# Causal attention: triangular masks taken from TensorE and given to GpSimd and VectorE

## The reference, cut to what matters

```python
q = (x @ Wq.T).reshape(B, S, H, hd).transpose(0, 2, 1, 3)   # k and v alike
scores = jnp.einsum('bhcd,bhsd->bhcs', qi, k) * scale
mask = kpos[None, :] <= qpos[:, None]
scores = jnp.where(mask, scores, jnp.finfo(scores.dtype).min)
p = jax.nn.softmax(scores, axis=-1)
return (None, jnp.einsum('bhcs,bhsd->bhcd', p, v))
```

## Time and profile before

| | |
|---|---|
| median of 3 executions | 2668.89 us (2668.31 to 9096.91) |
| span of the profiled execution | 2692.8 us |
| TensorE / VectorE / ScalarE / GpSimd busy | 91% / 69% / 52% / 30% |
| attention: head and groups | 151 to 224 us, 224 to 1156 us |

### The profile page before, as it was taken

One profiled execution on the slowest core, in us unless ns is written; L12 is line 12 of the kernel. 1 busy time (PEld: TensorE's weight loads), 2 busy tenths in 40 slices (PEclk: granted clock), 3 DMA queues, 4 the chain that ended last, 5 costly groups with the idle time before them and its releaser, 6 DMA issues. The chain is left out here.

```text
span 2692.8 us, 51134 instructions
## 1 busy us (share of the span) xinstructions
PE 2451.3 (91%) x16420; PEld 1589.0 (59%) x16420; DVE 1846.2 (69%) x3682; ACT 1406.8 (52%) x2776; POOL 815.1 (30%) x647
## 2 busy tenths in 40 slices
PE   5648999999999999969977599999999999999999
PEld 4512333333333333358866477777777777777777
DVE  7757877877787777424438476777667767766776
ACT  3404655656565566755634255555555555555554
POOL 1070000000000000014425355554455555444553
PEclk9858999999999999989988699999999999999999
DMA  4574041321404040033257000000000000000000
GB/s 135 191 170 65 5 62 26 41 52 16 61 6 62 6 60 5 7 127 133 102 177 241 18 13 12 11 13 13 13 13 13 9 11 13 13 13 13 13 9 9
DMA packets 189865, 132.85 MB, mean 49 GB/s; under 512 B 99857, under 2 KB 177687, under 8 KB 189712
## 3 DMA queue, kind: packets, MB, share of 16 engines
q1 hardware_dynamic: 160048, 100.06, 15.4%
q10 hardware_dynamic: 24160, 14.16, 2.2%
q0 software_dynamic: 5504, 16.69, 1.7%
HBM read 84.43 MB, written 46.14 MB: 48 GB/s over the span
## 5 line engine op out<-in xcount | busy, mean ns | idle before, releaser
L859 DVE TENSOR_REDUCE a_best<-a_ring 128x1 f32<-128x512 f32 (+3 forms) x1280 | 700.9, 604 | 214.0 <-PE a_ring L721 123.0
L836 ACT ACTIVATE a_probs<-a_pss 128x1024 f32<-128x1024 f32 (+3 forms) x640 | 554.0, 895 | 452.6 <-PE a_pss L777 228.7
L721 PE MATMUL a_ring<-a_kb,a_qa 96*128 96x512 bf16 (+3 forms) x1280 | 453.0, 365 | 67.2 <-DVE a_best L859 32.3
L774 PE MATMUL a_pss<-a_qa,a_kb 99*128 99x512 bf16 (+3 forms) x1280 | 433.9, 353 | 15.6 <-issue 7.2
L1771 ACT ACTIVATE w_probs<-w_pss,w_top 128x256 f32<-128x256 f32 x512 | 239.0, 476 | 379.7 <-DVE w_top L1859 365.0
L1606 POOL TENSOR_TENSOR w_probs<-w_probs,w_inv 128x512 f32<-128x512 f32 x256 | 301.0, 1176 | 395.7 <-DVE w_inv L1865 386.3
L962 POOL TENSOR_TENSOR e_w_r<-e_w,e_w_r 128x1024 fp32r<-128x1024 f32 x28 | 67.0, 2402 | 1032.7 <-ACT e_w_r L1035 1032.7
L1629 PE MATMUL w_psw<-wqkv,w_xr 128*128 128x512 f32 x1152 | 301.5, 398 | 11.6 <-POOL w_xr L1563 11.6
L774 PEld LDWEIGHTS a_pss<-a_qa,a_kb 99*128 99x128 bf16 x1280 | 123.5, 98 | 302.6 <-ACT a_probs L836 224.5
L792 PE MATMUL a_acc<-a_probs,a_vg 128*32 128x512 f32 (+3 forms) x2560 | 299.9, 541 | 0.1
L1669 PE MATMUL w_pss<-w_kd,w_qt 128*128 128x256 f32 x1536 | 278.4, 310 | 0.0
(11 more groups left out here) (223 smaller groups left out, 3771.2 us busy)
## 6 DMA issues: line engine op xcount, KB each, us to landing
e_w<-in_w SPq DMA_DIRECT2D x16, 1024.0 KB, 7.9
qk_parts<-p_parts SPq DMA_DIRECT2D x32, 384.0 KB, 3.7
a_qa<-qk_parts SPq DMA_DIRECT2D x192, 64.0 KB, 2.5
a_kb<-qk_parts SPq DMA_DIRECT2D x42, 256.0 KB, 9.5
p_xin<-in_x SPq DMA_DIRECT2D x8, 512.0 KB, 5.4
v_rows<-p_vout SPq DMA_DIRECT2D x8, 512.0 KB, 5.1
a_vg<-v_rows SPq DMA_DIRECT2D x32, 128.0 KB, 9.1
expert_in<-zero POOLq DMA_DIRECT2D x16, 256.0 KB, 8.3
```

Source lines behind the costliest of these rows:

```text
L721: ins = pe.matmul(bank[:, 0:keys], qa[u][0:QR, i // TC, h, (i % TC) * P:(i % TC + 1) * P], kb[u][0:QR, h, k * CH:k * CH + keys], start=Tru ...
L774: ins = pe.matmul(pss[idx % 2][:, e, lo:CH], kb[u][0:MR, h, j * P:(j + 1) * P], qa[u][0:MR, c, h, lo:CH], start=True, stop=(j < TC * c))
L836: act.activation(probs[:, idx % 4, :, lo:CH], pss[idx % 2][:, :, lo:CH], ACT.Exp).then_inc(exp_done, 1)
L859: vec.tensor_reduce(best[:, i // TC, h * TC + i % TC, k:k + 1], bank[:, 0:keys], X, ALU.max).then_inc(ring_taken, 1)
```

## The change

Masking leaves TensorE in both places.

- `mask_kq` is gone. Scores on the diagonal are exponentiated unmasked, and GpSimd then sets the entries of future keys in `probs` to zero with `affine_select`, one per pair of heads (2 x 128 columns), behind a one-element add that carries the wait for the exponential. Products on the diagonal wait for `future_cleared` instead of `exp_done`.
- The maxima's diagonal block is masked on VectorE: a reduction over the columns ahead of the block (one column where there are none), then `tensor_tensor_reduce`: PSUM block plus `mask_qk` (now fp32), maximum over it into a fifth column of `best`, its elementwise output written back to the bank. `best` is set to a lowest value at the start, and `split` reduces all five columns.
- `KEPT = 2` names the number of key tiles that `probs` holds; its size is as before.

```diff
+            for g, i, u, order in groups(pool):
+                idx = 0
+                for s in order:
+                    if s[0] == "S" and s[3] % 2 == 1:
+                        _, c, j, h = s
+                        if j >= TC * c:
+                            lo, slot = (j - TC * c) * P, idx % (KEPT * GH // 2)
+                            pool.wait_ge(exp_done, primed + g * n_s + idx + 1)
+                            pool.tensor_tensor(spare[:, slot:slot + 1], keep["zero"][:, 0:1], keep["zero"][:, 0:1], ALU.add)
+                            seen = probs[:, slot, :, lo:lo + P]
+                            pool.affine_select(out=seen, in_=seen, compare_op=ALU.is_ge, fill=0.0, base=0,
+                                               pattern=[[0, 2], [1, P]], channel_multiplier=-1).then_inc(future_cleared, 1)
+                        idx += 1
...
-                ins = pe.matmul(bank[:, 0:keys], qa[u][0:QR, i // TC, h, (i % TC) * P:(i % TC + 1) * P],
-                                kb[u][0:QR, h, k * CH:k * CH + keys], start=True, stop=not diagonal)
-                if diagonal:
-                    ins = pe.matmul(bank[:, keys - P:keys], keep["identity16"][:, :], keep["mask_qk"][:, :],
-                                    start=False, stop=True)
-                ins.then_inc(ring_full, 1)
+                pe.matmul(bank[:, 0:keys], qa[u][0:QR, i // TC, h, (i % TC) * P:(i % TC + 1) * P],
+                          kb[u][0:QR, h, k * CH:k * CH + keys], start=True, stop=True).then_inc(ring_full, 1)
...
-                                        qa[u][0:MR, c, h, lo:CH], start=True, stop=(j < TC * c))
-                        if j >= TC * c:
-                            ins = pe.matmul(pss[idx % 2][:, e, lo:lo + P], keep["identity16"][:, :],
-                                            keep["mask_kq"][:, :], start=False, stop=True)
+                                        qa[u][0:MR, c, h, lo:CH], start=True, stop=True)
...
-                        pe.wait_ge(exp_done, primed + g * n_s + 2 * pv + 2)
+                        if j < TC * c:
+                            pe.wait_ge(exp_done, primed + g * n_s + 2 * pv + 2)
+                        else:
+                            pe.wait_ge(future_cleared, g * n_diagonal + GH // 2 * (j + 1))
...
-                vec.tensor_reduce(best[:, i // TC, h * TC + i % TC, k:k + 1], bank[:, 0:keys], X, ALU.max
-                                  ).then_inc(ring_taken, 1)
+                found = best[:, i // TC, h * TC + i % TC, :]
+                if k < i // TC:
+                    vec.tensor_reduce(found[:, k:k + 1], bank[:, 0:keys], X, ALU.max).then_inc(ring_taken, 1)
+                else:
+                    own = slice(keys - P, keys)
+                    into = own if keys > P else slice(P, 2 * P)
+                    vec.tensor_reduce(found[:, k:k + 1], bank[:, 0:max(keys - P, 1)], X, ALU.max)
+                    vec.tensor_tensor_reduce(out=bank[:, into], in0=bank[:, own], in1=keep["mask_qk"][:, :], scale=1.0,
+                                             scalar=LOWEST, op0=ALU.add, op1=ALU.max, accum_out=found[:, QC:QC + 1]
+                                             ).then_inc(ring_taken, 1)
...
-                ch.link(vec.tensor_reduce(neg[:, :], best[:, c, :, 0:c + 1], X, ALU.max, negate=True))
+                ch.link(vec.tensor_reduce(neg[:, :], best[:, c, :, :], X, ALU.max, negate=True))
```

More of the change, by code:

```diff
@@ L36 @@
 NEG = -1e30
+LOWEST = -3.0e38
 HD = D // H
@@ L123, in _ @@
                                        fill=0.0, base=0, pattern=[[1, P]], channel_multiplier=-1))
-            ch.link(pool.memset(keep["zero16"][:, :], 0.0))
-            ch.link(pool.affine_select(out=keep["mask_qk"][:, :], in_=keep["zero16"][:, :], compare_op=ALU.is_ge,
+            ch.link(pool.memset(keep["zero32"][:, :], 0.0))
+            ch.link(pool.affine_select(out=keep["mask_qk"][:, :], in_=keep["zero32"][:, :], compare_op=ALU.is_ge,
                                        fill=NEG, base=0, pattern=[[-1, P]], channel_multiplier=1))
-            ch.link(pool.affine_select(out=keep["mask_kq"][:, :], in_=keep["zero16"][:, :], compare_op=ALU.is_ge,
-                                       fill=NEG, base=0, pattern=[[1, P]], channel_multiplier=-1))
             ch.link(pool.iota(keep["expert"][:, :, :], pattern=[[1, E], [0, NT]], base=0, channel_multiplier=0,
@@ L576 @@
 LEAD = 0.5
+KEPT = 2
 def stage_attention(nc, io, keep, dram):
@@ L586, in stage_attention @@
     n_pv = sum(u[0] == "PV" for u in steps)
+    n_diagonal = QC * TC * GH // 2
     parts_q, parts_k = (0, 0, 1, 1, 0, 2), (0, 1, 0, 1, 2, 0)
@@ L593, in stage_attention @@
         vg = [st.sb(f"vg{u}", [P, KT, GH, 32]) for u in range(2)]
-        probs = st.sb("probs", [P, 4, 2, CH])
-        best = st.sb("best", [P, QC, GH * TC, QC])
+        probs = st.sb("probs", [P, KEPT * GH // 2, 2, CH])
+        best = st.sb("best", [P, QC, GH * TC, QC + 1])
         neg = st.sb("neg", [P, GH * TC])
@@ L599, in stage_attention @@
         neg_rows = st.sb("neg_rows", [3 * GH * TC, 2, P], BF16)
+        spare = st.sb("spare", [P, KEPT * GH // 2])
         sums = st.sb("sums", [P, CH])
@@ L616, in stage_attention @@
         o_stored = [st.sem(f"o_stored{c}") for c in range(2)]
+        future_cleared = st.sem("future_cleared")
         dve_step = st.sem("dve_step")
@@ L717, in a_step @@
                 keys = min(CH, (i + 1) * P - k * CH)
-                diagonal = k == i // TC
                 wait(pe, ring_taken, r + 1 - RING)
-                ins = pe.matmul(bank[:, 0:keys], qa[u][0:QR, i // TC, h, (i % TC) * P:(i % TC + 1) * P],
-                                kb[u][0:QR, h, k * CH:k * CH + keys], start=True, stop=not diagonal)
-                if diagonal:
-                    ins = pe.matmul(bank[:, keys - P:keys], keep["identity16"][:, :], keep["mask_qk"][:, :],
-                                    start=False, stop=True)
-                ins.then_inc(ring_full, 1)
+                pe.matmul(bank[:, 0:keys], qa[u][0:QR, i // TC, h, (i % TC) * P:(i % TC + 1) * P],
+                          kb[u][0:QR, h, k * CH:k * CH + keys], start=True, stop=True).then_inc(ring_full, 1)
             def m_turn(n, r, bank):
@@ L833, in _ @@
                         act.wait_ge(s_ready, g * n_s + idx + 1)
[L835 to L836 removed]
+                        act.wait_ge(pv_done, primed + g * n_pv + max(idx // 2 - KEPT + 1, 0))
+                        act.activation(probs[:, idx % (KEPT * GH // 2), :, lo:CH], pss[idx % 2][:, :, lo:CH], ACT.Exp).then_inc(exp_done, 1)
                         idx += 1
@@ L876, in take_rows @@
                 vec.tensor_copy(neg_rows[:, c % 2, :], bank[0:3 * GH * TC, 0:P // 2].bitcast(BF16)).then_inc(ring_taken, 1)
+            vec.memset(best[:, :, :, :], LOWEST)
             ch.link(vec.memset(neg_parts[:, :, :], 0.0))
@@ L1928, in make_program @@
             "ones16": st.sb("ones16", [P, P], BF16),
-            "zero16": st.sb("zero16", [P, P], BF16),
+            "zero32": st.sb("zero32", [P, P]),
             "before16": st.sb("before16", [P, P], BF16),
-            "mask_qk": st.sb("mask_qk", [P, P], BF16),
-            "mask_kq": st.sb("mask_kq", [P, P], BF16),
+            "mask_qk": st.sb("mask_qk", [P, P]),
             "expert": st.sb("expert", [P, E, NT]),
```

4 lines of the change are left out of this document (1 added, 3 removed).

## The result

The changed kernel took 2684.9 us (median of 4 executions, 2682.3 to 2687.4) against 2668.6 for the kernel before (median of 4, with the one at 9096.91 us that stood far off from the start): a ratio of 1.0062, 95% interval 1.0047 to 1.0077. That is 16 us slower, within 2%. The forecast was 2670, one us slower, with a range of 2632 to 2715. The class and the range held; the sum missed 15 us, and what it consists of is the subject of the rest.

What follows compares the result with a forecast made beforehand. TensorE was taken to bound the attention groups, with VectorE behind it. The terms 12.6 + 2.5 - 3.4 - 9 - 3.7 gave -1, one us lost: median from 2668.9 to 2670 us, range 2632 to 2715.

Steps and rivals of the forecast that it cites:

- Removed from TensorE: Attention stage: 1024 mask matmuls of 0.058 us go, 59 us or 7.4 us per group, the ceiling of the gain.
- step sum: Attention groups: the larger of TensorE's and VectorE's time, summed over 40 steps between products; 110.5 us before, 108.7 after.
- r: Added VectorE time for the accumulator read-out in each diagonal unit of the maxima; taken as 0.1 us, between 0 and 0.33.
- Added to VectorE: Diagonal units of the maxima: one instruction becomes three, 0.166 us more each, 64 units and 10.6 us per group.
- second case: Read-out and select both hidden, no stall at products: 31 us gained, 2638 us; chance 0.22.
- (0,3): Step before the product of query chunk 0, key tile 3: VectorE-bound, 3.54 us before and 3.71 after, so slower.
- fourth case: The three VectorE instructions of a diagonal unit do not overlap: 0.30 us added per unit, 2711 us; chance 0.11.
- Moved to GpSimd: Diagonal products wait for add-and-select pairs, 0.65 us path: stalls at group ends 6.4 us, last group 2.4, together 9 lost.
- GpSimd's queue is free: GpSimd is busy 0.00 us from 224 on, its scatters being issued in the head; no loss was charged.
- Head: Row maxima made ahead of the groups: 44 diagonal units cost VectorE 7.3 us more, half charged, 3.7 us lost.
- A wait that takes part back: TensorE's four waits for rows of maxima, 5.8 us in all, each lengthen by 0.85 us: 3.4 us lost.
- Signs: Profile after: TensorE about 60 us less busy, waits at reductions' ring, 0.8 us group-end stalls, rows' wait near 2.5 us.

Runs made afterwards that it cites:

- best: Kernel before with score masks on GpSimd except each group's last key tile, scatters between later groups' selects, values' loads behind rows of maxima; 2645.9 us, ratio 0.9912.
- scores only: Changed kernel with the maxima's mask matmuls back on TensorE and single reductions on VectorE, GpSimd still clearing probabilities; 2684.6 us, ratio 1.0043 to the kernel before.
- maxima only: Changed kernel with score masks back on TensorE and products waiting for exponentials, maxima still masked on VectorE; 2680.6 us, ratio 1.0028 to the kernel before.
- scatters later: Changed kernel with GpSimd's scatters issued between the selects of the last two groups; 2679.1 us, ratio 1.0022 to the kernel before.
- all three: Changed kernel with scatters late, values' loads behind rows of maxima, and score masks of each group's last key tile back on TensorE; 2651.5 us, ratio 0.9916.
- second profile of the kernel before: The kernel before, unedited, profiled once more; 2667.2 us in one execution, span 2665.6 us.

## Why the prediction was right in its class and 15 us off in its sum

**Removed from TensorE: right in kind.** TensorE's busy time per group fell by 5.8 us (7.4 forecast). That a freed microsecond isn't a gained one was the core of the step sum, and the kernel without masks shows it: 4.5 of 7.4. The sum had 4.9 at r = 0, where each diagonal unit still costs VectorE 0.065. With nothing at all added to VectorE it comes to about 6, which I worked out afterwards from the same costs. So it promises too much even where the change adds no work.

**Added to VectorE: r was too high, and the sum too kind.** Here is one unit, as VectorE's timeline:

```profile
195.71 0.15 DVE L878 TENSOR_REDUCE a_best<-a_ring 128x1 f32<-128x1 f32 x1
195.78 0.29 DVE L879 CUSTOM_DVE_ANT_0 a_ring<-a_ring,mask_qk 128x128 f32<-128x128 f32 x1
195.98 0.14 DVE L879 DVE_READ_ACCUMULATOR2_ANT a_best<- 128x1 f32 x1
195.98 1.28 DVE L874 TENSOR_REDUCE a_best<-a_ring 128x1 f32<-128x512 f32 x2
```

The add-and-maximum is followed 0.20 us after its start, like a plain reduction of 128 columns, and the next reduction starts with the read-out: r is 0.01, not 0.1. A diagonal unit costs 0.07 us more, not 0.166. By the step sum this should have given 4.9 us per group (the second case), less 0.8 at its end. It gave 1.6 with that stall, 2.4 without. So two errors met: r was too high, and the sum promised too much for its r. That the forecast of 1.8 stands so near the 2.4 is luck. The step that failed in the sum is that it takes the larger of two engines for each step alone. Time that TensorE gains in steps of its own is handed back in the next step that VectorE bounds: (0,1) and (0,2) got 0.23 and 0.30 shorter and (0,3) 0.39 longer, although the one diagonal unit in it costs only 0.07 more; *best*, in which VectorE does exactly what it did before, has -0.23, -0.24 and +0.33 there. By the time between two products, (2,7) rose by 0.58 and (3,6) by 0.32. For (2,7) the sum, worked out again with the measured r, has 0.53 less: this one step is some two fifths of what it promised too much. The sum should have carried VectorE's backlog from step to step. That this carry is the cause is my reading of these steps; no run isolates it.

The Trainium skill ("VectorE: DVE Perf Modes", section Two Vector instructions with no wait between them) treats an operation with an accumulator output as two instructions, the main one and a read. The trace agrees: 512 of each. Its section The DRAIN you can't avoid, by which the fourth case went, does not hold for these reductions: the next one starts before the end of the last (0.20 us after the start of a 0.29 us operation), and the case of 2711 did not come. The page itself lets operations that are not held start earlier.

**Moved to GpSimd: price right, queue wrong.** The forecast for a pair was an add of 0.1 and a select of 0.40. Measured are 0.193 and 0.406, 0.52 from pair to pair since they overlap. At a group's end:

```profile
930.62 0.19 POOL L684 TENSOR_TENSOR a_spare<-zero 128x1 f32<-128x1 f32 x1 [0.39 <-ACT a_probs L849]
930.76 0.41 POOL L686 TENSOR_SCALAR_AFFINE_SELECT a_probs<-a_probs 128x256 f32<-128x256 f32 x1
931.14 0.19 POOL L684 TENSOR_TENSOR a_spare<-zero 128x1 f32<-128x1 f32 x1
931.28 0.41 POOL L686 TENSOR_SCALAR_AFFINE_SELECT a_probs<-a_probs 128x256 f32<-128x256 f32 x1
...
931.74 0.42 PE L805 MATMUL a_acc<-a_probs,a_vg 128*32 128x128 f32 x8 [0.81 <-POOL a_probs L686]
```

A stall of 0.81 us in seven groups, 0.50 in the last: the forecast was 0.8. Behind the first group's start no product inside the chunks of the seven groups waits, as said, but for 0.14 us at the last but one, (3,14); the last group, for which 2.4 us of such waits were forecast, took 95.5 us for 96.3, and its trace has two such waits of 0.36 us each besides the one at its end. What failed is the sentence "GpSimd's queue is free": it is true from 224 us on, in a profile in which the products began at 229.6. It needed the question whether the first select comes after the last scatter in an ordinary execution too. The answer costs some 8 us at the first product (6.9 of them a wait in the changed kernel) and 2 to 3 in the two steps behind it. Nothing in the list of rivals had this.

**Head: mis-sized.** 3.7 forecast, 9.3 measured. The backlog alone makes nearly all of it: *scores only*, in which VectorE does what it did before, has 9.1. VectorE's part shows only where no backlog hides it: 3.0 us in *maxima only*, 1.7 in *scatters later*, 2.0 between *all three* and *best*.

**A wait that takes part back: the term that was mis-sized.** 3.4 forecast, 20.5 measured in its three steps. The direction and the place were right, and so was the wait itself, nearly: the waits for rows grew from 4.7 to 10.7 us, by 6.0. The term that was missing is the clock. The prediction took it at the groups' 0.99 throughout, also behind the longer waits. None of the three waits in the second profile of the kernel before (1.3, 1.5 and 2.0 us) was followed by a lower granted clock, and all four in the changed kernel (2.2 to 3.0 us) were. Step (2,0) then takes 4.22 us for 2.93, (2,1) 0.4 to 1.1 us more, and the scores behind the wait start 0.43 us apart for 0.22. This makes some 14 of the 20.5 us; the remaining 0.6 is work.

How long a wait must be is not settled by these runs. In *maxima only* waits of 1.7 and 2.0 us were followed by a granted clock of 0.50, and waits of 1.4 and 1.9 us were not. In *scatters later* the clock read 0.50 already during a wait of 4.4 us and was back at 1.00 some 4 us after it, so that step (2,0) took 2.91 us.

The wait itself grew for two reasons. TensorE comes 1.3 us sooner, where the prediction had 0.85. And in group 1 the kernel before had no wait at all (2.48 us in step (1,7), against 4.03, 3.84 and 4.50 in groups 3, 5 and 6), because there the rows had landed before TensorE came; in the changed kernel they landed 2.0 us later in that group, and the step takes 6.8 us. In the others they landed 0.0 and 0.5 us later and 1.2 sooner, counted from the end of the group before. SyncE did issue the first of the three row loads later in groups 1, 3 and 5, at 31.0 to 31.8 us for 29.4 to 29.8, because the loads ahead of it took longer, but little of that reached the last landing in groups 3 and 5. Why the same loads take longer is not settled. They do so in the kernel without masks too (15.4 to 15.6 us for the values in these three groups, 12.1 to 14.3 before), so neither GpSimd's selects nor VectorE's reads cause it; a different execution of one kernel differs as well.

**Signs.** Of what the prediction said would show it right, the rows' wait "near 2.5 us" was 3.0 at the longest, and the stalls at the ring and at the group's end are there. TensorE's busy time fell by 28 us only (2452.3 in the second profile of before, 2424.0 after), of the forecast 60; part of what it does ran at the lower clock and counts double there. VectorE's operations are closer together than said.

## What to carry to other kernels

An engine that is idle in the bulk of a stage is not free at its start: look up what the last instruction of the earlier work on that queue is and whether the first new one comes after it, in an execution whose head you trust. And where several loads stand ahead of a small, urgent one in a queue, making the compute faster buys a wait, and the wait can cost more than its length when TensorE's clock is lower behind it (10.7 us of waits and 14 us of slower work here). One move in SyncE's program, values behind rows, was worth more (24 us) than the change itself (nothing). When two engines trade work step by step, carry the backlog of each from step to step rather than take a maximum for each.

## What the runs showed of the hardware that was not expected

- After TensorE stood for 3.0 us its granted clock was 0.50 for some 9 us of nearly full work. The length of the wait alone doesn't decide it: behind 1.7 us in *maxima only* the clock read 0.50 as well, behind 2.0 us in the kernel before it stayed at 1.00. In the changed kernel the slower work behind four waits (14 us) cost more than the waits (10.7 us).
- A reduction with an accumulator over two sources costs VectorE 0.206 us from start to start at 128 columns (a plain one 0.198), although its recorded length is 289 ns; its read-out, recorded as 141 ns, adds nothing when a reduction follows.
- A one-element add on GpSimd takes 193 ns, a select over 256 elements 406 ns, and one pair behind another 0.52 us.
